# One channel's statistics in halves, the kernel's powers and a table load begun earlier, and small copies moved to ScalarE, in a one-block vision tower

## What is computed

```python
h = _layernorm(p, ln1_w, ln1_b)                    # p: patches, 576 rows of 768
h = _layernorm(jnp.einsum('bsp,pd->bsd', h, W) + b, ln2_w, ln2_b)
out = jnp.concatenate([cls_tok, h], axis=1) + pos
# state-space block: rms norm with gamma, W_in, a causal convolution, then
sigA, sigB, sigC = jax.nn.sigmoid(A), jax.nn.sigmoid(Bp), jax.nn.sigmoid(C)
h = sigA * h + sigB * xt[:, :, None]               # a scan over 37 tokens
y = jnp.einsum('ben,en->be', h, sigC)
out = y @ W_out.T + b_out                          # + residual
# feed-forward: gelu(x @ W1 + b1) @ W2 + b2 for 31 patch tokens of each image,
# pairs of experts with a two-way gate for the 6 first tokens
```

## Time and profile before

| | us |
|---|---|
| median of 3 runs | 101.78 |
| lowest and highest | 100.31, 101.84 |
| the profiled execution | 99.3 |
| its span | 97.6 |
| busy in the span: PE, DVE, ACT, POOL | 84.1, 65.1, 39.6, 37.3 |
| chain that ended last, by engine | PE 43%, DVE 29%, DMA 7%, SP's queue 6%, issue 5%, ACT 5% |

### The profile page before, as it was taken

How to read it: one execution, slowest core, us unless ns; L and a number is a source line. 1 busy time by engine, 2 the same in 40 slices (tenths; PEclk the granted TensorE clock), 3 DMA queues, 4 the chain that set the end, 5 groups by cost and what they waited for, 6 DMA issues and landing times.

```text
span 97.6 us, 1829 instructions
## 1 busy us (share of the span) xinstructions
PE 84.1 (86%) x583; PEld 71.2 (73%) x583; DVE 65.1 (67%) x216; ACT 39.6 (41%) x105; POOL 37.3 (38%) x97
## 2 busy tenths in 40 slices
PE   1979999979967955999799899979989999999920
PEld 1958899969946935999697699966568537887810
DVE  3969979957999999999978797785000307048310
ACT  2352598820634681335650122312975005850000
POOL 6803359999893264009644004244410400000000
PEclk9999999999999999999999999999999999999999
DMA  1999995999999899999921000010211310000211
GB/s 10 275 269 228 234 258 167 236 177 255 315 279 257 145 282 221 222 326 329 313 74 51 1 3 27 14 57 7 60 45 28 87 39 0 0 0 0 75 44 39
DMA packets 14412, 13.28 MB, mean 136 GB/s; under 512 B 4024, under 2 KB 12450, under 8 KB 14402
## 3 DMA queue, kind: packets, MB, share of 16 engines
q1 hardware_dynamic: 13410, 13.15, 52.7%
q10 hardware_dynamic: 992, 0.01, 0.6%
HBM read 12.24 MB, written 0.91 MB: 135 GB/s over the span
## 4 chain that ended last, share of the span: by engine, by line
PE 43%; DVE 29%; DMA 7%; SPq 6%; issue 5%; ACT 5%; DVEq 0%
PE ps L1093 41%; DMA pixel_area<-in_x_dram 7%; SPq L316 3%; DVE h L896 3%; DVE xT_area L932 2%; DVE st L836 2%; DVE xT_area L935 2%; DVE xs L914 2%; DVE st L902 2%; DVE h L883 2%; DVE st L873 2%; SPq L330 2%; ACT pixel_area L737 2%; DVE xT_area L941 1%; ACT L737 1%
## 5 line engine op out<-in xcount | busy, mean ns | idle before, releaser
L1093 PE MATMUL ps<-W_area,xT_area 128*108 128x192 f32 (+2 forms) x72 | 13.5, 329 | 0.4 <-ACT xT_area L575 0.3
L1093 PEld LDWEIGHTS ps<-W_area,xT_area 128*108 128x108 f32 (+2 forms) x72 | 10.9, 167 | 1.0 <-issue 0.8
L1093 PE MATMUL ps<-WoutT,xT_area 128*108 128x192 f32 (+1 forms) x42 | 7.6, 328 | 1.6 <-DVE xT_area L941 1.6
L1093 PE MATMUL ps<-W_sb,pixel_area 128*124 128x192 f32 x48 | 8.8, 332 | 0.0
L1093 PEld LDWEIGHTS ps<-W_sb,pixel_area 128*124 128x124 f32 x48 | 7.7, 187 | 1.2 <-issue 1.2
L532 POOL TENSOR_TENSOR rs<-ve,neg_half 108x1 f32<-108x1 f32 (+2 forms) x6 | 3.6, 598 | 12.7 <-DVE ve L959 12.7
L1093 PEld LDWEIGHTS ps<-WoutT,xT_area 128*108 128x108 f32 (+1 forms) x42 | 6.8, 177 | 2.0 <-DVE xT_area L941 2.0
L575 ACT ACTIVATE xT_area<-ps 120x192 f32<-120x192 f32 (+2 forms) x6 | 2.6, 437 | 12.3 <-PE ps L1093 12.3
L1093 PE MATMUL ps<-x4TT,W_sb 128*128 128x248 f32 x24 | 5.8, 384 | 1.2 <-ACT pixel_area L737 0.7
L575 ACT ACTIVATE xT_area<-ps,ln_col 128x576 f32<-128x576 f32 (+1 forms) x6 | 4.8, 807 | 4.6 <-PE ps L1110 4.6
L836 DVE BATCH_NORM_STATS2 st<-pixel_area 96x6 f32<-96x256 f32 x18 | 6.1, 407 | 0.6 <-DMA pixel_area<-in_x_dram 0.6
(11 more groups left out here) (214 smaller groups left out, 199.6 us busy)
## 6 DMA issues: line engine op xcount, KB each, us to landing
line_area<-in_L_ffn_A_W_dram SPq DMA_DIRECT2D x5, 576.0 KB, 9.9
A_sb<-in_L_ffn_A_W_dram SPq DMA_DIRECT2D x5, 384.0 KB, 4.7
pixel_area<-in_x_dram SPq DMA_DIRECT2D x6, 288.0 KB, 6.3
A1R<-in_L_ffn_A_W_dram SPq DMA_DIRECT2D x10, 96.0 KB, 4.6
W_area<-in_L_tok_W_dram SPq DMA_DIRECT2D x2, 288.0 KB, 5.0
W_sb<-in_L_ffn_moe_W_dram SPq DMA_DIRECT2D x1, 576.0 KB, 7.6
W_sb<-in_L_ffn_moe_W_dram SPq DMA_DIRECT2D x1, 384.0 KB, 6.1
W1R<-in_L_ffn_moe_W_dram SPq DMA_DIRECT2D x2, 192.0 KB, 6.2
```

The lines of the kernel that those rows point to most:

```text
L1093: return t.matmul(out_, lhsT, rhs, start=start, stop=stop, skip_group_check=True)
```

## The change

It moves the loads of A, Bp and C from SP to ScalarE's queue, ahead of the ln1 loads; sigmoid and the sqrt table load follow at once. The first line-up is shared by VectorE and GpSimd. GpSimd starts the powers behind it and cuts them into pieces of eight, with its other line-ups between. The last channel's statistics are taken in two halves. `Fk` is written later (`kernel_table`), the first `fold` comes ahead of `product(3, [4, 5])`. ScalarE writes all second copies of `xs` and `x4` of groups 0 and 1, GpSimd takes rs2 of groups 2 to 5. The transposes of `x4` no longer use a second copy; `put_x4T` writes three parts. The gelu table is loaded ahead of time. The diff below is cut to these parts, in the order SP, GpSimd, ScalarE, VectorE, TensorE.

```diff
-    WARM, WARM2 = 7, 2
+    WARM, WARM2 = 10, 2
...
             load_x(1, 1)
-            for i, v in enumerate((A, Bp, C)):
-                sp.dma_start(ssm[:, i].rearrange("p e n -> p (e n)"), v.rearrange("(p e) n -> p (e n)", e=ET)
-                             ).then_inc(l_ssm, 16)
             load_x(2, 0)
...
-            line_up(1)
-            line_up(3)
+            pool.wait_ge(l_x[0][0], 16)
+            g_.tensor_scalar(xr[:, 0, 3:].rearrange("p n (y w) -> p n y w", y=HB),
+                             x_pix[:, 0, 0:HB].rearrange("p y n w -> p n y w")[:, 3:],
+                             1.0, 1.0, MUL, MUL).then_inc(x0p_ready, 1)
...
             pool.wait_ge(sig_ready, 1)
...
+                for c0 in range(0, n, 8):
+                    c1 = min(c0 + 8, n)
+                    ins = g_.tensor_tensor(powr[:, cur + c0:cur + c1, :], powr[:, c0:c1, :],
+                                           base.unsqueeze(1).broadcast_to([128, c1 - c0, ET * NST]), MUL)
+                    k = step(ins)
+                    if cur + c1 == 24:
+                        line_up(3)
                 cur, i = cur + n, i + 1
                 if cur == 8:
+                    line_up(1)
+                if cur == T:
                     line_up(5)
...
+            def root2(g):
+                n = ROWS[g]
+                pool.wait_ge(var2, g + 1)
+                g_.tensor_tensor(rs2[0:n, g:g + 1], ve2[0:n, g:g + 1], neg_half[0:n, :], ALU.pow
+                                 ).then_inc(rs2p_ready, 1)
...
-            for g in range(4):
-                residual_scales(g)
+            residual_scales(0)
+            root2(2)
+            residual_scales(1)
+            root2(3)
+            residual_scales(2)
+            root2(4)
+            residual_scales(3)
+            root2(5)
             add_cls()
...
+            for i, v in enumerate((A, Bp, C)):
+                act.dma_start(ssm[:, i].rearrange("p e n -> p (e n)"), v.rearrange("(p e) n -> p (e n)", e=ET)
+                              ).then_inc(l_ssm, 16)
+            act.wait_ge(const_ready, 3)
+            a_.activation(table_row[:, 0:1], ones[:, 0:1], ACT.Sigmoid)
             act.dma_start(ln1_col[:, 0], ln1_w.rearrange("(h p c) -> p h c", h=H2, c=NC)).then_inc(l_ln1, 16)
             act.dma_start(ln1_col[:, 1], ln1_b.rearrange("(h p c) -> p h c", h=H2, c=NC)).then_inc(l_ln1, 16)
+            act.wait_ge(l_ssm, 48)
+            a_.activation(ssm[:, :, :, :], ssm[:, :, :, :], ACT.Sigmoid).then_inc(sig_ready, 1)
+            a_.activation(table_row[:, 1:2], ones[:, 0:1], ACT.Sqrt)
...
+            def put_x4(g):
+                n = FULL[g]
+                act.wait_ge(rs4_ready, g + 1)
...
+                copy(x4[0:n, g, 0:D], h3[0:n, g, :], bias=nm4[0:n, g:g + 1], scale=rs4[0:n, g:g + 1]
+                     ).then_inc(x4a_ready, 1)
...
             put_dT(4)
             again_xs(5)
+            act.wait_ge(rc_ready, NG)
+            a_.activation(table_row[:, 2:3], ones[:, 0:1], ACT.Gelu)
             put_r(3)
...
+                parts = [(slice(0, 128), slice(0, 128), 0), (slice(0, DR), slice(0, DR), 1),
+                         (slice(DR, 128), slice(0, DR), 1)]
...
-            for c in range(NC):
+            for c in range(2):
...
+            for hh in range(H2):
+                dve.wait_ge(l_x[2][hh], 16)
+                for nw in range(NW):
+                    k = step(v.bn_stats(st1[:, nw, 2 + hh, :], x_pix[:, 2, HB * hh:HB * (hh + 1), nw, :]))
...
-                if g < 2:
-                    v.tensor_scalar(xs[0:n, g, D:], h2[0:n, g, DL:], ag3[0:n, g, 0:1], s3[0:n, g, 1:2], SUB, MUL
-                                    ).then_inc(xd_ready, 1)
...
-            apply4(0)
-            apply4(1)
# TensorE
             turn(5)
-            product(2, [4, 5])
-            turn_Win()
+            product(4, [0, 1])
...
-            product(4, [0, 1])
+            turn_Win()
             product(5, [0, 1])
-            product(3, [4, 5])
-            turn_Win_rest()
+            product(2, [4, 5])
             fold([0, 1])
+            product(3, [4, 5])
+            turn_Win_rest()
```

More of the change, by code:

```diff
@@ L606, in _ @@
             put_xT(1)
+            act.dma_start(gcol[:, 0:1], gamma[0:DL].unsqueeze(1)).then_inc(l_gam, 16)
+            for i in range(2):
+                act.dma_start(gcol[DR * i:DR * (i + 1), 1:2], gamma[DL:D].unsqueeze(1)).then_inc(l_gam, 16)
             line_up(2)
             put_xT(2)
-            act.wait_ge(l_ssm, 48)
-            a_.activation(ssm[:, :, :, :], ssm[:, :, :, :], ACT.Sigmoid).then_inc(sig_ready, 1)
             line_up(4)
@@ L718, in _ @@
             put_r(5)
+            put_x4(0)
             put_P(3)
+            put_x4(1)
             def put_x4T(g):
@@ L723, in put_x4T @@
                 src = x4bank(g)
[L724 to L731 removed]
+                parts = [(slice(0, 128), slice(0, 128), 0), (slice(0, DR), slice(0, DR), 1),
+                         (slice(DR, 128), slice(0, DR), 1)]
+                for to, of, s in parts:
+                    if g == 0:
+                        copy(x4TT[to, s, :, 0], src[of, s, CLS:CLS + 1].broadcast_to([128 if s == 0 else DR, NB])
+                             ).then_inc(x4T_cls, 1)
+                    ins = copy(x4TT[to, s, B0[g]:B0[g] + NBG[g], 1:T],
+                               src[of, s, 0:ROWS[g]].rearrange("p (b t) -> p b t", t=S))
+                    if to.start == DR:
+                        ins.then_inc(x4T_ready, 1)
             def put_hid(s, j):
@@ L978, in _ @@
             spread(1)
+            kernel_table()
             center(2)
```

140 lines of the change are left out of this document (73 added, 67 removed).

## The result

The changed kernel takes 108.08 us (median of 4 runs, 107.93 to 108.54), beside 101.05 for the kernel before on the same chip (4 runs, 99.23 to 101.84): a ratio of 1.084, with an interval of 1.073 to 1.096. (All ratios here are taken over undisturbed runs alone, so they can stand off the ratio of the medians, which is 1.070 here.) It is slower by 7 us; the prediction said 101.7 and a range up to 104.0. The profiled run took 108.01 us, with a span of 106.3 where the kernel before had 97.6, so the two traces differ by 8.7.

What follows compares the result with a forecast made beforehand. A chain of waits bounds the kernel: SP's issues and x loads to 14.0 us, mostly VectorE to 47.0, then TensorE. Terms +1.1, −0.75 and −0.4 sum to about 0, so 101.7 us, range 99.7 to 104.0.

Steps and rivals of the forecast that it cites:

- ln1's landing: Start of the kernel: ln1_b, issued at 3.1 on ScalarE's queue, lands at 8.7 us instead of 5.0.
- The step that failed: VectorE before the first fold: from its half of xT at 8.7 to the first statistics at 12.1 us.
- part 2: First fold to transform(5): 25.4 us instead of 26.18, a gain of 0.75 (bounds 0.3 and 1.1).
- rival D: GpSimd's additions before TensorE's u_rep matmuls stretch: +0.5 us at most, inside the forecast, no separate chance.
- part 1: Start to the first fold: fold at 22.35 us, 1.1 later than before.
- Rival A: ln1 issues wait for the table load, ln1_b lands at about 10.3: 103.3 us, 104.3 with slow TensorE start; chance 0.28.
- Part 3: transform(5) to the end: table load before the gelus goes, extra x4TT copies cost; up(2) at 70.8, gain 0.4 us.
- 0.22 for slower: Whole kernel slower by about 2%: worse half of the late-ln1 rival, run spread on its other half; chance 0.22.

Runs made afterwards that it cites:

- the filler: Idle TensorE multiplications added to the changed kernel: 23 where it waits for ms (106.3 us); or, with statistics first, 14 where it waits for ln1 (100.91 us).
- polynomial early: Changed kernel with VectorE's nine polynomial steps for the sine table ahead of its wait for ln1: 102.39 us, ratio 1.019.
- GpSimd waiting: Changed kernel with GpSimd's line-ups 1 and 3 first and its powers waiting until VectorE's polynomial is done: 101.93 us, ratio 1.024.
- statistics first: Changed kernel with VectorE's statistics and ms ahead of the polynomial, and F's rows behind fold_rows: 101.74 us, ratio 1.011.
- the old start: Changed kernel with the previous kernel's start (loads, ScalarE's and GpSimd's order, polynomial), the later parts of the change kept: 101.21 us, ratio 0.997.
- the early sigmoid: Kernel with the old start and two copies, ScalarE's sigmoid moved from behind put_xT(2) to behind put_xT(1): 101.25 us, ratio 0.990.
- two copies: Kernel with the old start, x4TT filled by two copies a group instead of three, second half's columns written twice as before: 99.55 us, ratio 0.980.
- the gelu table alone: Kernel before the change with only the gelu table load moved early, behind again_xs(5): 100.29 us, ratio 0.998.

## Why the prediction was wrong

**ln1's landing was right.** Predicted 8.7, read 8.81: issued at 3.09, beside the table load, it took 5.7. C was predicted at 6.5 and landed at 5.49. The first product was predicted at 9.35, and came at 9.48.

```profile
2.29 1.28 ACT L610 ACT_TABLE_LOAD   x1 [2.29 <-issue]
2.67 0.39 ACTq L611 DMA_DIRECT2D ln_col<-in_L_tok_ln_w_dram  x1
3.09 0.51 ACTq L612 DMA_DIRECT2D ln_col<-in_L_tok_ln_b_dram  x1
...
5.49 0.32 ACT L614 ACTIVATE ssm<-ssm 128x144 f32<-128x144 f32 x1 [1.70 <-DMA ssm<-in_L_attn_C_dram]
```

**The step that failed** is the sentence "From it to the first statistics at 9.44 were 2.9 us; two more table operations (0.23 each, 0.5 with gaps) now lie between: 12.1." It took the durations from a stretch in which GpSimd did one line-up (0.84 us), and used them for one in which I myself had GpSimd at work throughout: part 2 says "POOL's long chain starts at 7". The stretch took 10.14 us and not 3.4. Those 6.75 us are most of the 8.4 by which the fold came later than forecast; the half clock behind the stall, about 1.8 by the filler, is the rest. The two ways of removing the overlap (polynomial early, GpSimd waiting) and the way of hiding it (statistics first) each gave most of it back.

That chance was in the prediction as a remark: "probably stalls beside POOL (h2 of group 1 took 0.69, as h2 of others 0.42)", and as rival D, "+0.5 at most". The trace of before had what was needed to size it: one multiply-add in five at 0.73 us beside a line-up, Fk at 1.63 us where the changed kernel, with GpSimd idle, has 0.16, and the power chain's own operations of 1 to 2 us. A chain of nine short operations, each waiting for the one before, may pay that at each: L874, L878, the five of L881 and L883 take 9.28 us in the changed kernel and 1.93 at the durations that they have elsewhere (0.20, 0.20, 1.30, 0.23).

The Trainium skill (SBUF — State Buffer, "SBUF: two separate sides") says that VectorE, in an operation with two SBUF inputs or in a 2-port mode, and GpSimd exclude each other from a shared pair of ports for whole instructions. The trace agrees on the whole: operations with two inputs and the short SBUF copies are stretched (0.20 to 1.00 us), statistics with one input are not (405 ns beside GpSimd's powers with the statistics first; 404 in the kernel before from 9.4 to 11, where GpSimd does nothing). It goes beyond it in one thing. The multiply-add of 2797 ns starts at 14.4 and ends at 17.2, past the end of GpSimd's line-up at 15.0 and the whole 2066 ns addition behind it:

```profile
L881 DVE SCALAR_TENSOR_TENSOR tb_n<-tb_n,tb_s x2: 1166/1982/2797, 14.4 to 17.2; 128x72 f32<-128x72 f32 x2
```

```profile
L499 POOL TENSOR_TENSOR powr_area<-powr_area x1: 2066/2066/2066, 15.0 to 15.0; 128x888 f32<-128x888 f32 x1
```

It waited for two operations in a row, and so did the first of the five: 1758 ns from 11.62, over a line-up (11.50 to 12.33) and a power (12.29 to 13.28). So here GpSimd's longest operation was no upper bound of a stall. That it is the ports that are waited for is the skill's account; the runs show the stall and its conditions.

**The rest of part 1.** TensorE's transposes were to wait until 20.1; they waited until 26.6. Halves of statistics: predicted 0.22 each from start to start and 2.6 for twelve; measured 0.20 and 2.39. From the ms transposes to the fold 4.11 us, 3.5 before, at half the clock: the other part of the loss that the prediction didn't have. Rival A had the slow start of TensorE behind an idle stretch, sized at 1. With the full clock it is 1.3 less from the first product to the fold (13.34 with the filler, 14.67 without), and in the changed kernel itself it is hidden behind the stall.

**Part 2 had the right number, partly by luck.** 25.53 where 25.4 was predicted; TensorE's wait for u_rep 0.71 where 1.1 was. Its mechanism was only half right: with the old start VectorE has the same fewer operations and the stretch takes 26.96, longer than before. Only where Kk ends early does the gain appear (25.29 with the early sigmoid, where the wait for Kk is gone). The prediction counted GpSimd's early chain only for the stalls that it saves VectorE.

**Part 3 had the right mechanism and came out with the other sign.** A gain of 0.4 was predicted, a loss of 0.34 measured. Moving the gelu table is worth 0.75 (0.68 predicted). Three copies instead of two cost 0.85 at up(2) (24.11 against 23.26), and not 0.3; that is the mis-sized term. A further 0.24 ahead of up(0) stays with two copies (23.26 against 23.02 with the gelu table alone) and wasn't traced. On the copies, rows of after show 0.57 us for a group's three, and `up(0)` and `up(1)` both wait for them.

```profile
73.48 1.95 PE L1149 MATMUL ps<-x4TT,W_sb 128*128 128x248 f32 x8 [0.75 <-ACT x4TT L604]
...
78.25 1.12 PE L1149 MATMUL ps<-x4TT,W_sb 128*128 128x248 f32 x4 [0.38 <-ACT x4TT L604]
```

**The chances.** 0.22 for slower was too little, and the range ended at 104.0, below the 104.3 that rival A itself gave with a slow start. A stall between VectorE and GpSimd was left at one term inside the forecast where it was a rival with a place (the polynomial), a price (up to the length of GpSimd's chain, 5.9 to 23.2 us) and a point from which it decides (VectorE's statistics ending behind TensorE's products, at 21.1 in this trace).

## What to carry to other kernels

When a change moves two engines against each other in time, check each moved operation's duration against what its new neighbour does there: a duration read from a quiet stretch isn't a price for a busy one. A chain of short dependent operations with two SBUF inputs on VectorE should stand where GpSimd is idle or has only short operations, or behind what the critical path needs; work with one input (statistics) stood beside GpSimd here at no cost. A load put behind others on a queue costs what its consumer's engine loses in order and in clock, here up to 4.0 us for 3.9 us of lateness.
